# A graph network on one core: the transposed count matrix made by transposing DMAs during the attention, and the remainders of z formed by TensorE

## The reference

```python
# attention, per head: z = W h;  e = leaky(a_src.z[src] + a_dst.z[dst])
ex = jnp.exp(e_h - m[dst])
den = jax.ops.segment_sum(ex, dst, num_segments=N)
alpha = ex / jnp.maximum(den[dst], jnp.float32(1e-16))
return jax.ops.segment_sum(alpha[:, None] * z_h[src], dst, num_segments=N)
...
# convolution: two segment sums, along the edges one way and then the other
m = jax.ops.segment_sum(xt[src], dst, num_segments=n) * Binv[:, None]
out = jax.ops.segment_sum(m[dst], src, num_segments=n) * Dinv[:, None]
```

## Time and profile before

| | |
|---|---|
| median of 3 runs | 1759.34 us |
| the profiled execution: its own time | 1760.4 us |
| its span | 1758.7 us |
| count phase, first to last one-hot tile | 71.96 to 323.35 us |
| attention | 338 to 810 us |
| busy over the span: PE, DVE, ACT | 90%, 61%, 62% |

### The profile page before, as it was taken

The page is one execution under the profiler, slowest core; times in us unless marked ns, Lnnn a source line. Parts: engine busy times, 40 slices in busy tenths (PEclk is TensorE's granted clock), DMA queues, the critical chain, the costliest instruction groups (busy, mean ns, idle before and its releaser), DMA issues. The chain is left out here.

```text
span 1758.7 us, 35425 instructions
## 1 busy us (share of the span) xinstructions
PE 1583.0 (90%) x11857; PEld 1391.8 (79%) x11857; DVE 1069.2 (61%) x1881; ACT 1097.1 (62%) x2034; POOL 79.8 (5%) x116
## 2 busy tenths in 40 slices
PE   5677777699999999997999799999999999999697
PEld 4566666699999999996666699997789999777465
DVE  5798888589999999997455411123232112677662
ACT  2577777788888888884333466565655555567221
POOL 3000000000000000002000100000000000111213
PEclk9788888699999999999999899999999999999899
DMA  7325555264040212203000144445545444657211
GB/s 207 94 72 177 161 161 163 70 167 116 16 104 16 71 42 58 55 1 88 1 0 0 41 126 125 120 112 126 141 127 125 123 124 107 157 148 174 68 32 52
DMA packets 137571, 170.14 MB, mean 97 GB/s; under 512 B 20374, under 2 KB 129099, under 8 KB 137448
## 3 DMA queue, kind: packets, MB, share of 16 engines
q1 hardware_dynamic: 127538, 155.71, 33.6%
q0 software_dynamic: 6368, 9.36, 2.1%
q10 hardware_dynamic: 3542, 3.46, 0.8%
HBM read 114.58 MB, written 53.86 MB: 96 GB/s over the span
## 5 line engine op out<-in xcount | busy, mean ns | idle before, releaser
L1605 PE MATMUL ps_sets<-arena,kinds_mem 125*125 125x195 bf16 (+1 forms) x2500 | 447.9, 247 | 24.7 <-DVE kinds_mem L1364 16.7
L1348 ACT ACTIVATE kinds_mem<-ed_rows,es_mask 125x625 bf16<-125x625 f32 x500 | 367.2, 810 | 59.9 <-PE ps_sets L1611 32.1
L1611 PE MATMUL ps_sets<-arena,kinds_mem 125*125 125x195 bf16 (+1 forms) x2300 | 397.6, 249 | 0.0
L1605 PEld LDWEIGHTS ps_sets<-arena,kinds_mem 125*125 125x125 bf16 x2500 | 342.9, 137 | 31.6 <-DVE kinds_mem L1364 23.5
L2794 ACT ACTIVATE onewide<-ring 125x625 fp32r (+1 forms) x325 | 222.5, 720 | 168.7 <-PE oneps L2511 95.3
L1611 PEld LDWEIGHTS ps_sets<-arena,kinds_mem 125*125 125x125 bf16 x2300 | 308.7, 134 | 0.0
L2483 PE MATMUL oneps<-onewide,parts_a 125*128 125x376 f32 (+1 forms) x2000 | 293.8, 308 | 8.2 <-DVEq L2574 8.1
L2483 PEld LDWEIGHTS oneps<-onewide,parts_a 125*128 125x128 f32 x2000 | 291.5, 190 | 9.6 <-DVEq L2572 8.4
L2511 PE MATMUL oneps<-oneparts_b,onewide 125*125 125x512 f32 x1000 | 234.6, 395 | 0.0
L2511 PEld LDWEIGHTS oneps<-oneparts_b,onewide 125*125 125x125 f32 x1000 | 184.5, 185 | 48.6 <-DVE onefull L2646 1.9
L1356 DVE TENSOR_TENSOR kinds_mem<-kinds_mem,blk 125x2500 bf16<-125x2500 bf16 x120 | 182.4, 1520 | 34.9 <-ACT kinds_mem L1348 29.2
(11 more groups left out here) (449 smaller groups left out, 1876.2 us busy)
## 6 DMA issues: line engine op xcount, KB each, us to landing
ring<-counts SPq DMA_DIRECT2D x50, 683.6 KB
ring<-countsT SPq DMA_DIRECT2D x40, 683.6 KB
countsT<-kinds_mem SPq DMA_DIRECT2D x25, 683.6 KB
blk<-counts SPq DMA_DIRECT2D x20, 546.9 KB
counts<-blk SPq DMA_DIRECT2D x3, 3418.0 KB
counts<-kinds_mem SPq DMA_DIRECT2D x2, 3418.0 KB
ed_rows<-ed_dram SPq DMA_DIRECT2D x16, 273.4 KB
ring<-countsT SPq DMA_DIRECT2D x10, 410.2 KB
```

The lines of the kernel that those rows point to most:

```text
L1348: return k.nc.scalar.activation(kinds_of(k)[:, slot, 0, :], k.ed_b[:, h, :], ACT.Relu, scale=MASK_SCALE, bias=k.es_mask[:, t, h:h + 1])
L1605: t_.matmul(out[0], kind[0], z[0], start=(t == 0), stop=False)
L1611: last = t_.matmul(out[1], kind[1], z[1], start=False, stop=(t == T - 1))
```

## The change

`countsT` is no longer made in the count phase. PE's transposes, ACT's `tr_out` and SP's store behind each tile are gone. In the attention SP makes it instead, from `counts` in DRAM: 125 units, each a transposing DMA of 640 rows by 128 columns into one of six slots in SBUF (`fetch_transposed`) and, three units later, two plain DMAs of the 125 rows by 625 columns that are wanted, to `countsT` (`store_transposed`). They stand in twelve batches of 11 units behind the `load_ed` of heads 0 to 2 (`stage`); `ST_EACH = 0` puts none in the count phase. SP's loop over blocks is written out.

In the count phase `full` stays on DVE. The remainders are now formed by PE in PSUM (`rest`): `ident` times `full` in fp32, minus the parts so far by a bf16 matrix `minus_eye`, in two banks of 260 columns; ACT rounds all three parts (`part`), the last two out of PSUM. SP waits for the landing of a block's store before it goes on.

```diff
+ST_ROWS = 640
+ST_SLOTS = 6
+ST_UNITS = U * U * U
+ST_EACH = 0
+ST_COUNT = (U - 1) * ST_EACH
+ST_HEAD = 11
+ST_LAG = 3
...
-TR_AFTER = [(0, 1), (2,), (3, 4), (5,), (6,)]
...
+def staged_from(n):
+
+    j, rest = divmod(n, U * U)
+    block, w = divmod(rest, U)
+    row = min(block * QB, N - ST_ROWS)
+    col = (j * U + w) * P - (128 - P if w == U - 1 else 0)
+    return row, col, block * QB - row, (j * U + w) * P - col, (j * U + w) * P, block * QB
+
+
+def fetch_transposed(k, sp, n, slot):
+
+    row, col = staged_from(n)[0:2]
+    first = k.counts[row, col:col + 128]
+    if n >= ST_SLOTS:
+        sp.wait_ge(k.st_out[n % ST_SLOTS], 32 * (n // ST_SLOTS))
+    sp.dma_start_transpose(slot, bass.AP(first.tensor, first.offset, [[N, ST_ROWS], [1, 128]])).then_inc(k.st_in[n % ST_SLOTS], 16)
+
+
+def store_transposed(k, sp, n, slot):
+
+    off_row, off_col, d0, s0 = staged_from(n)[2:]
+    sp.wait_ge(k.st_in[n % ST_SLOTS], 16 * (n // ST_SLOTS + 1))
+    for lo_, hi_ in SPLIT:
+        sp.dma_start(k.countsT[d0 + lo_:d0 + hi_, s0:s0 + QB],
+                     slot[off_col + lo_:off_col + hi_, off_row:off_row + QB]).then_inc(k.st_out[n % ST_SLOTS], 16)
...
+                    if not isinstance(t, int):
+
+                        dve.wait_ge(part_done[0], t)
+                        dve.wait_ge(rest_done[1], t)
...
-                    v.drain()
-
-                def without_first(t):
...
-                def third(t):
...
-                        if u == 3 and not first:
-                            third(i - 1)
-                        if u == 4:
-                            without_first(i)
...
-                def tr_out(i, banks):
...
+                def part(t, c):
+
+                    if c == 0:
+                        act.wait_ge(scaled, t + 1)
+                        src = full[:, :, :, :].rearrange("p h e d -> p (h e) d")
+                        a.activation(zpart(t, c), src, ACT.Copy).then_inc(part_done[c], 1)
+                    else:
+                        act.wait_ge(rest_done[c - 1], t + 1)
+                        a.activation(zpart(t, c).rearrange("p (b x) d -> p b x d", b=2),
+                                     ps_r[0:P, :, 0:HALF_Z].rearrange("p b (x d) -> p b x d", d=D1), ACT.Copy).then_inc(part_done[c], 1)
...
-                        act.wait_ge(tr_stored, 32 * i)
...
-                            tr_out(i - 1, TR_AFTER[u])
+                        if u % 2 == 0:
+                            part(i, u // 2)
...
-                def transposes(j, w, banks):
...
+                def rest(i, c):
+
+                    if c == 0:
+                        pe.wait_ge(scaled, i + 1)
+                        if not isinstance(i, int):
+                            pe.wait_ge(part_done[2], i)
+                    pe.wait_ge(part_done[c], i + 1)
+                    for b in range(2):
+                        t_.matmul(ps_r[0:P, b, 0:HALF_Z], k.ident[0:P, 0:P],
+                                  full[:, 2 * b:2 * b + 2, :, :].rearrange("p h e d -> p (h e d)"), start=True, stop=False)
+                        for part in range(c + 1):
+                            last = t_.matmul(ps_r[0:P, b, 0:HALF_Z], minus_eye, zpart(i, part)[:, 4 * b:4 * b + 4, :],
+                                             start=False, stop=(part == c))
+                    last.then_inc(rest_done[c], 1)
+
+                def tile(i):
                     for u in range(U):
                         histogram(i, u)
-                        if before:
-                            if u == 0:
-
-                                pe.wait_ge(blk_done, U * i + U)
-                            transposes(*before, TR_AFTER[u])
-
-                for j in range(U):
-                    tile(j, 0, (j - 1, U - 1) if j else None)
-                    with pe.Fori(1, U) as w:
-                        tile(j, w, (j, w - 1))
-                pe.wait_ge(blk_done, U * T + U)
-                transposes(U - 1, U - 1, range(NTB))
+                        if u in (1, 3):
+                            rest(i, u // 2)
...
-                        sp.wait_ge(tr_done, NTB * (i + 1) + 2)
-                        sp.wait_ge(tr_stored, 32 * i + 64)
-                        for lo_, hi_ in SPLIT:
-                            sp.dma_start(k.countsT.rearrange("(t p) s -> t p s", p=P)[bass.ds(i, 1), lo_:hi_, :].rearrange("a p s -> (a p) s"),
-                                         tr[lo_:hi_, bass.ds(i % 2, 1), :].rearrange("p a s -> p (a s)")).then_inc(tr_stored, 16)
...
+                for j in range(U - 1):
+                    sp.wait_ge(blk_done, U * U * (j + 1) + U)
+                    sp.wait_ge(blk_stored, 32 * j + 64)
+                    for lo_, hi_ in SPLIT:
+                        sp.dma_start(k.counts[:, j * QB:(j + 1) * QB].rearrange("(t p) d -> p t d", p=P)[lo_:hi_],
+                                     blk[j % 2][lo_:hi_, :, :]).then_inc(blk_stored, 16)
+                    sp.wait_ge(blk_stored, 32 * j + 96)
...
+        def free_slot(n):
+
+            s = n % ST_SLOTS
+            if s < 4:
+                return k.cut_mem[:, s * ST_ROWS:(s + 1) * ST_ROWS]
+            at = 2 * sums_at + 4 * U * W3 + 10 + (s - 4) * ST_ROWS
...
+                def stage(some):
+                    for n in some:
+                        if n < ST_UNITS:
+                            fetch_transposed(k, sp, n, free_slot(n))
+                        if ST_COUNT <= n - ST_LAG < ST_UNITS:
+                            store_transposed(k, sp, n - ST_LAG, free_slot(n - ST_LAG))
+
+                wait_staged(k, sp, ST_COUNT)
...
-                with sp.Fori(1, U) as b:
+                for b in range(1, U):
                     for h in range(HEADS - 1):
 
                         sp.wait_ge(mask_done, T * (HEADS * (b - 1) + h + 1))
                         load_ed(b - 1, h)
+                        at = ST_COUNT + ST_HEAD * ((HEADS - 1) * (b - 1) + h)
+                        stage(range(at, at + ST_HEAD))
...
+                stage(range(ST_COUNT + ST_HEAD * (HEADS - 1) * (U - 1), ST_UNITS + ST_LAG))
+                wait_staged(k, sp, ST_UNITS)
```

More of the change, by code:

```diff
@@ L634, in zrows, with staged, wait_staged, count_slot @@
     return k.arena[:, :].rearrange("p (t h e s) -> p t h e s", t=T, h=HEADS, e=2)
+def staged_from(n):
[16 more added lines that the diff above has]
+                     slot[off_col + lo_:off_col + hi_, off_row:off_row + QB]).then_inc(k.st_out[n % ST_SLOTS], 16)
+def staged(n):
+    return [len(range(slot, n, ST_SLOTS)) for slot in range(ST_SLOTS)]
+def wait_staged(k, sp, n):
+    for slot, uses in enumerate(staged(n)):
+        if uses:
+            sp.wait_ge(k.st_out[slot], 32 * uses)
+def count_slot(k, n):
+    at = T * QB + 7 + (n % ST_SLOTS) * ST_ROWS
+    return k.kinds_all[:, at:at + ST_ROWS]
 def count_phase(k):
@@ L729, in _ @@
                     hots(i, False)
-                third(T - 1)
+                v.drain()
                 v.memset(zrows(k)[:, :, 0, :, W3:WP].rearrange("p t e a -> p t (e a)"), 1.0)
@@ L826, in histogram @@
                     last.then_inc(hist_done, 1)
-                def transposes(j, w, banks):
-                    for r in banks:
-                        pe.wait_ge(tr_done, NTB * (U * j + w) + r + 1 + (1 if r == 0 else 0))
-                        for s in range(min(TQ, T - r * TQ)):
-                            last = t_.matmul(ps_tr[0:P, r % 2, s * P:(s + 1) * P],
-                                             blk[j % 2][:, r * TQ + s, bass.ds(w * P, P)],
-                                             k.ident_bf[0:P, 0:P], start=True, stop=True)
-                        last.then_inc(tr_psum, 1)
-                def tile(j, w, before):
-                    i = U * j + w
+                def rest(i, c):
[12 more added lines that the diff above has]
+                def tile(i):
                     for u in range(U):
                         histogram(i, u)
-                        if before:
-                            if u == 0:
-                                pe.wait_ge(blk_done, U * i + U)
-                            transposes(*before, TR_AFTER[u])
-                for j in range(U):
-                    tile(j, 0, (j - 1, U - 1) if j else None)
-                    with pe.Fori(1, U) as w:
-                        tile(j, w, (j, w - 1))
-                pe.wait_ge(blk_done, U * T + U)
-                transposes(U - 1, U - 1, range(NTB))
+                        if u in (1, 3):
+                            rest(i, u // 2)
+                pe.wait_ge(eye_set, 1)
+                tile(0)
+                with pe.Fori(1, T) as i:
+                    tile(i)
             @block.sync
@@ L858, in _ @@
                 sp.sem_inc(blk_stored, 64)
-                sp.sem_inc(tr_stored, 64)
                 for lo_, hi_ in SPLIT:
@@ L3163, in program @@
         k.blk_stored, k.ed_first = sem("blk_stored"), sem("ed_first")
```

(3 more changed lines are left out.)

71 lines of the change are left out of this document (23 added, 48 removed).

## The result

The changed kernel takes **1798.14 us** (median of 4 runs, 1795.9 to 1801.7) against 1759.82 for the kernel before on the same chip: a ratio of 1.0219, 95% interval 1.0205 to 1.0233. It is slower by 38 us. The profiled execution took 1798.43 us, 38.0 above the 1760.4 of before.

What follows compares the result with a forecast made beforehand. DVE was taken to pace the count phase, PE the attention. The count phase's -16, its tail's -2.5 and the attention's +12 summed to -6.5 us, so 1753 us by the median; range 1730 to 1805.

Steps and rivals of the forecast that it cites:

- rival D: Attention: a unit costs 1.8 to 2.6 us by SP's issue, making the kernel slower by 4 to 60 us; chance 0.28.
- I take 1.5: Attention, SP's queue: 1.5 us a unit, so block 1's 33 units overrun their 35.4 us by 14.1.
- Blocks 2 to 4: nothing: Attention: after block 1, the units delay no later block's loads of counts, 0 us.
- I give back 2: Attention, block 1: slack in PE and DVE recovers 2 us of the 14.1 us lateness, leaving +12.
- The prices by bytes (1.1) and by packets (3.5): Attention: alternative costs of a unit, 1.1 us from bytes at 293 GB/s, 3.5 us from 765 packets at 74 ns.
- F: Attention: packets make a unit 3.5 us and SP the bound, +180 and -18.5, about 1920 us; chance 0.08.
- the loop through PE and ACT: Count phase: this loop, 8.6 us a tile at 2.4 GHz, sets the pace instead of DVE's 7.8.
- I take a little less time at the lower level than now, 30%: Count phase: PE at 1.2 GHz for 30% of the time, giving 9.4 us a tile and 16 us less.
- A: The forecast: a unit 1.3 to 1.65 us, block 1 late 6 to 17, count phase 12 to 25 shorter; chance 0.38.
- B: Units fit at 1.1 us or less and the clock stays up more: 20 to 36 us faster; chance 0.09.
- C: Count-phase gain and attention loss cancel within 0.2%, with a unit at 1.6 to 1.8 us; chance 0.13.
- E: Count phase: PE at 1.2 GHz half the time, 10.0 us a tile, no gain there: 1768 us; chance 0.04.

Runs made afterwards that it cites:

- loads_pool: The changed kernel with the loads of counts issued from GpSimd's queue instead of SP's: 1717.49 us, ratio 0.9756 to the kernel before.
- old_z: no_units with both subtractions for z on VectorE again, and the second rounding by ScalarE from its result: 1747.72 us.
- lag_4: The changed kernel with each unit stored four units behind its fetch instead of three: 1804.07 us.
- spread: The changed kernel with units on SP's queue in another order, fewer per head, some behind loads of counts, the rest in the last block: 1717.26 us, ratio 0.9746.
- old_z_hot: old_z with twelve fp32 products a tile added on TensorE that nobody reads: 1749.92 us.
- no_units: The changed kernel without the transposing units and their stores, the convolutions reading counts in place of countsT: 1716.98 us.

## Why the prediction was wrong, step by step

I said 1753 us, faster than before; it is 1798. The range held it, and rival D, at 0.28, was what happened.

- **The step that failed: "I take 1.5, near the issue of three DMAs and the landing over three, as the transposing DMA has one instruction and short regular rows."** It measured 2.53 us in block 1. Of the three prices, issue ruled, and in it the transposing DMA was put near a plain one; it takes 1.13 us where a plain one takes 0.36 to 0.5. The two stores take 1.02 and not 0.77. So a regular unit is 2.24 us. The upper bound by issue, 2.4, was nearly right, for a wrong reason: 320 rows cost as much as 640. The working also had no term for the first four fetches, which are some 7 us longer behind the loading of x. By my own formula 33 x 2.53 - 35.4 = 48 us; the row has 49.8. The budget of 35.4 us was right within a few us.
- **"Blocks 2 to 4: nothing"** follows from the same term; it was 15.6, 14.2 and 1.3. D was short here too. I had counted the third batch alone, and at 2.53 us a unit that gives 11 x 2.53 - 20.1 = 7.7. The first two batches (28 us against their 24) overrun as well and start the third late: its `ed` rows start at 510.4 us, only 18 before DVE is free at 544.20 - 15.59 = 528.6. All three batches together give 33 x 2.53 - 24 - 24 - 20.1 = 15.4, which is what the rows have. (D's own "at 2.3 by 9 each" is a slip: the third batch alone gives 5.2 there, all three 7.8.)
- **"I give back 2"** for slack: nothing came back.
- **The prices by bytes (1.1) and by packets (3.5)** fall, and F with them: a unit takes 2.53 us, and loads_pool moves the same bytes for 0.5 us.
- **The Trainium skill's 1309 ns** for a 128x128 square by DMA ("VectorE: DVE Perf Modes", section on the three transpose paths) does not hold here as a price for each square: a fetch of five squares is issued in 1.13 us and lands 2.9 us after. Its comparison of the two paths, 390 ns on TensorE against 1309 by DMA, pointed the right way. The Trainium skill's 261 GB/s ("DMA: Bandwidth & Descriptors", section on latency and other measured facts; 0.63 us a fetch, an estimate from it) is not contradicted, and is not what a unit costs.
- **The count phase: the loop through PE and ACT was right, the clock was not.** I said 8.6 us at 2.4 GHz; it is 8.28 (DVE's scaling starts at 166.14 and, 13 tiles later, at 273.81 us), and DVE waits "at `scale` for the second remainder", as written. But "I take a little less time at the lower level than now, 30%" was a guess, and the phase's clock is 0.99. With the clock never down my working gives 215 us, -36; the loop's own error is the other 7 of the 27 us by which -16 was short of -43.2. The 70% that I had worked out for TensorE's load could not carry that guess: load and clock were 73% and 0.82 before, old_z stands at 1.2 GHz with 139 of 201 us busy, and the changed kernel at 2.4 with 154 of 201. What sets the level in the changed kernel was not tried by itself.
- **The tail**, -2.5, measured -2.0. Rivals A, B, C and E fall: the unit is too dear for the first three, and the clock went up.

Put together, my sum with the clock at 0.99 and the measured waits would have been 1760.4 - 36 - 2.5 + 81 = 1803. The two terms had opposite signs, and I took a middle value for each. That the range held the result is luck in part: both errors are large (27 us too little gained, 69 us too little lost), and they offset each other.

Open: why a few issues on SP take 2 to 2.9 us (two of 7.3 and 8.3 in loads_pool), what the first four fetches wait for, and the 6 us of lag_4.

## What to carry to other kernels

Price a DMA by what the issuing queue pays for it, by kind of instruction, as well as by bytes and packets; and ask of each in-order queue what stands behind the added work and when it is due. 125 transposing units cost 81 us ahead of loads that have a due time. They cost under 1 us behind or between the same loads on the same queue (spread), or with the loads on another queue (loads_pool). Where an engine gets work that feeds back into the loop, place the feedback steps as early as their inputs allow: moving two roundings and one product by a step or two was worth 13 us.

## What the hardware showed that I had not expected

- A transposing DMA occupies SP for 1.13 us with 640 rows of 128 columns and for 1.20 with 320; a plain one of 128 rows 0.36, a store of 125 rows 0.47, two stores of 112 and 13 rows 1.02 behind a transposing DMA and 0.87 to 0.95 behind a plain one.
- TensorE's clock in the count phase was 0.50, 0.82, 0.92 and 0.99 in four kernels whose DVE or loop sets the pace: histograms alone (139.5 of 201 us busy), with transposes, with idle fp32 products (147.3), and with the remainders (153.8). With more work on TensorE its histograms were shorter: 316 ns a product in old_z, 237 in old_z_hot, 225 in the changed kernel.
- The DMA engines' share from 293 to 855 us is 0.23 in no_units and 0.66 in loads_pool, and the kernel's median time is the same within 0.5 us.
